# A gated cross-attention and FP4 feed-forward block on one core: gate and output projection computed with the weights stationary, turned back by PE, and the codes' casts given to DVE

## The chip, the cores and the metric

The kernel runs on one NeuronCore of a Trainium2 chip. The time is that of the device in microseconds (us), from start to end of the program. PE is TensorE, DVE is VectorE, ACT is ScalarE, POOL is GpSimd, SP is SyncE, whose queue issues the DMAs. PEld is PE's loading of the stationary operand.

## What is computed

```python
def _L0_xattn_ref(hidden_states, memory_tokens, memory_mask, norm_w, wq, wk, wv, wo, wg):
    x = rmsnorm(hidden_states, norm_w)
    q = (x @ wq.T).reshape(B, L, NH, HD)            # NH = 16 heads of HD = 32
    k = (memory_tokens @ wk.T).reshape(B, M, NH, HD)
    v = (memory_tokens @ wv.T).reshape(B, M, NH, HD)
    attn = jnp.einsum('blhd,bmhd->bhlm', q, k) * scale
    attn = jnp.where(memory_mask[:, None, None, :], attn, -jnp.inf)
    attn = jax.nn.softmax(attn, axis=-1)
    out = jnp.einsum('bhlm,bmhd->blhd', attn, v).reshape(B, L, C)
    out = out @ wo.T
    gate = jax.nn.sigmoid(x @ wg.T)
    return gate * out

def _L0_ffn_ref(x, ...):                            # weights are FP4 codes with group scales
    gate, up = halves of einsum('bsh,oh->bso', x, w_gu)
    h = jax.nn.silu(gate) * up
    y = jnp.einsum('bsi,hi->bsh', h, w_down)
    return y / jnp.sqrt(jnp.mean(y * y, axis=-1, keepdims=True) + EPS)

x = x + jnp.tanh(g_xattn[0]) * _L0_xattn_ref(_layernorm(x), ctx_2048, mask_BxS2_bk0, ...)
x = x + jnp.tanh(g_ffn[0]) * _L0_ffn_ref(_layernorm(x), ...)
```

There are 16 batches of 100 tokens of width 512, and 361 context tokens a batch, of which the mask leaves at most the last 96.

## The kernel before

**Split numbers.** Every fp32 operand of a product is kept as a high and a low part (fp32r, `_hi` and `_lo`), and a product is three passes: high by high, high by low, low by high. ACT copies the high part out of PSUM (`job_hi`), DVE subtracts it from the same bank and writes the low part (`job_lo`).

**Attention** takes four groups of NB = 4 batches, one after the other. A group is 16 steps, one for each head. In step i PE turns the probabilities of head i (`transpose_probs`, L1659), multiplies those of head i - 1 with the values (`attend`, L1673 and L1675), and in steps 2, 6, 10 and 14 computes the scores of the next four heads (`scores`). Beside that, each step does the jobs that the table `BESIDE` names for it, in its order, on PE, ACT and DVE alike:

- X0 to X3: the normalised tokens of batch n of the next group are turned (xT)
- Qn, Kn: 128 columns of the queries and keys of the group; W stationary (128 columns), tokens moving (400 of xT, 384 of the context)
- An, Bn: values for 128 context rows, half of the heads each
- Tn: the attention output of heads 4n to 4n + 3 is turned (oT)
- Gn: x @ wg for batch n, its 100 tokens stationary and 512 columns of wg moving, 12 matmuls; ACT then takes tanh of half of it into `gate[n]` (L902)
- On: the attention output of batch n by wo in the same manner, 12 matmuls (L1620, L1624). DVE then forms (gate + 1) * product (L1229) and that times a coefficient plus the residual (L1233), and SP stores it as x1.

A job's bank is in `BANK_OF` (and its variants for the first, third and last cycle); `open_bank` makes PE wait until the job before in that bank has been read. The loop over groups runs from step 6 of one group to step 5 of the next, three times, with steps 0 to 5 of group 0 ahead of it and steps 6 to 15 of group 3 behind it.

**FP4 weights** are decoded inside the three cycles of the loop, 6 pieces each (`KINDS = "uduudu"`). DVE does stages 0 to 2 (shift, mask, sign; L1317, L1326, L1333) for each, two stages a step behind `attn_sum`. Stage 3 of an up piece ("u", the codes of gate and up weights) is a cast of 128x1024 fp16 to fp32r by ACT (L953); stages 3 and 4 of a down piece ("d") are multiplications on POOL (L743). SP stores the result in DRAM scratch.

**Feed-forward.** Five groups (j) of 320 tokens, each 11 tiles (t) of 128 hidden columns. A tile is 16 matmuls for gate and up (L1771), whose banks ACT and DVE empty (L1037, L1395), POOL adds, and from j = 1 on the down products (L1784) of the group before. The first five tiles of j = 0 stand in steps 11 to 15 of the last attention group, the others in the order of `AT_LAST`, between the last O jobs. Tokens of the next j are normalised, turned in three pieces by PE (L1719), and split by ACT and DVE (L1367) within tiles of the present one; the first products of a j wait for the last split.

**POOL** also divides by the softmax sum (`attn_norm`, L733), takes rstd (L724) and forms the low part of the context of the next group (`ctx_lo`, L719), for which job K0 waits; ACT makes its high part at the steps of `CTX_AT`.

## Time and profile before

| | us |
|---|---|
| median of 3 runs | 585.15 (583.78 to 585.34) |
| the profiled execution, its own time | 583.25 |
| its span, first to last instruction | 581.4 |
| PE busy | 534.2 (92% of the span) |
| DVE busy | 431.1 (74%) |
| ACT busy | 347.9 (60%) |
| POOL busy | 295.7 (51%) |

A matmul's record holds its way through the array, so the records of neighbours overlap; what a matmul costs in a row of them is the distance from its start to the next one's start.

### The profile page before, as it was taken

Reading aid. Unit: us, or ns where it says so; the run is one execution under the profiler, and the core shown is the slowest. Engines: PE = TensorE matmul, PEld = TensorE weight load, DVE = VectorE, ACT = ScalarE, POOL = GpSimd, SP = SyncE. Lnnn points to the kernel's source line nnn. Section 1 sums busy time; section 2 is a strip of 40 time slices with the busy share of each in tenths; the row PEclk is TensorE's granted clock in tenths of the full one; section 3 lists DMA queues with packets and bytes.
Section 4 is the critical chain, followed back from the end, with each engine's and each line's share of the span. In section 5 each row is a group of like instructions: output and inputs, shape, how many; then the busy total and the mean of one; then the engine's idle time right before and its main releaser. Section 6 shows DMA issues by size and latency. Waiting matters only on the chain.

```text
span 581.4 us, 12493 instructions
## 1 busy us (share of the span) xinstructions
PE 534.2 (92%) x3962; PEld 468.0 (80%) x3962; DVE 431.1 (74%) x994; ACT 347.9 (60%) x948; POOL 295.7 (51%) x320
## 2 busy tenths in 40 slices
PE   2787988999899998999997898999999999999996
PEld 2687878988789887988886676888998988899983
DVE  6666868767688686896647987988897898867721
ACT  4677558645676446765467644676666667665610
POOL 6913373402735026441104854887776677866720
PEclk9998999999999999999999999999999999999998
DMA  6930146331464322432672027502110211011111
GB/s 223 340 118 0 56 130 184 135 135 49 147 168 159 117 65 93 147 132 92 220 277 76 2 61 238 195 0 83 38 36 2 83 37 37 2 37 37 37 64 32
DMA packets 27899, 59.37 MB, mean 102 GB/s; under 512 B 3656, under 2 KB 5832, under 8 KB 27848
## 3 DMA queue, kind: packets, MB, share of 16 engines
q1 hardware_dynamic: 27848, 58.76, 30.6%
q8 instruction: 23, 0.38, 0.3%
q14 instruction: 28, 0.23, 0.1%
HBM read 39.62 MB, written 19.14 MB: 101 GB/s over the span
## 4 chain that ended last, share of the span: by engine, by line
PE 64%; DVE 15%; issue 8%; ACT 8%; POOL 1%; DMA 1%; DVEq 0%; ACTq 0%; SPq 0%; POOLq 0%
PE bank L1771 18%; PE bank L1784 15%; PE bank L323 12%; PE bank L1620 5%; PE bank L1624 3%; PE bank L332 2%; ACT probs L928 2%; PE bank L1648 2%; DVE nmax L1206 2%; DVE vb_both L1174 2%; PE bank L1673 1%; PE bank L1659 1%; DVE part_gate L1395 1%; ACT vb_both L908 1%; DVE words L1317 1%
## 5 line engine op out<-in xcount | busy, mean ns | idle before, releaser
L1771 PE MATMUL bank<-mT_hi,wgu 128*128 128x320 f32 x440 | 138.3, 325 | 9.9 <-ACT part_up L1037 3.4
L1771 PE MATMUL bank<-mT_lo,wgu 128*128 128x320 f32 x440 | 131.2, 309 | 0.0
L733 POOL TENSOR_TENSOR o<-pv_sum,rinv 100x128 f32<-100x128 f32 x64 | 42.6, 666 | 147.4 <-DVE pv_sum L1223 147.2
L928 ACT ACTIVATE probs<-bank,nmax 100x96 f32<-100x96 f32 x256 | 66.6, 348 | 61.6 <-DVE nmax L1206 61.6
L1771 PEld LDWEIGHTS bank<-mT_hi,wgu 128*128 128x128 f32 x440 | 82.5, 188 | 23.5 <-ACT part_up L1037 5.2
L1771 PEld LDWEIGHTS bank<-mT_lo,wgu 128*128 128x128 f32 x440 | 82.7, 188 | 3.5
L805 POOL TENSOR_TENSOR part_gate<-part_gate 128x320 f32<-128x320 f32 x55 | 57.0, 1037 | 54.8 <-DVE part_gate L1395 54.8
L1037 ACT ACTIVATE part_up<-bank,scale 128x320 f32<-128x320 f32 x110 | 57.3, 522 | 39.9 <-PE bank L1771 39.6
L1395 DVE SCALAR_TENSOR_TENSOR part_up<-bank,scale,part_up 128x320 f32<-128x320 f32 x110 | 58.9, 546 | 20.0 <-ACT part_up L1037 18.5
L1037 ACT ACTIVATE part_gate<-bank,scale 128x320 f32<-128x320 f32 x110 | 52.1, 529 | 28.0 <-PE bank L1771 27.6
L1395 DVE SCALAR_TENSOR_TENSOR part_gate<-bank,scale,part_gate 128x320 f32<-128x320 f32 x110 | 55.4, 544 | 13.5 <-ACT part_gate L1037 11.8
L811 POOL TENSOR_TENSOR part_up<-part_up 128x320 f32<-128x320 f32 x55 | 57.4, 1044 | 8.7 <-DVE part_up L1395 7.1
L1784 PE MATMUL bank<-wdn_lo,hT_hi 128*128 128x512 f32 (+1 forms) x143 | 56.5, 395 | 0.0
L1784 PE MATMUL bank<-wdn_hi,hT_lo 128*128 128x512 f32 (+1 forms) x143 | 56.4, 395 | 0.0
L1784 PE MATMUL bank<-wdn_hi,hT_hi 128*128 128x512 f32 (+1 forms) x143 | 56.4, 394 | 0.0
L798 POOL TENSOR_TENSOR hT_lo<-hidden,hT_hi 128x320 fp32r<-128x320 f32 x55 | 50.4, 916 | 5.9 <-ACT hT_hi L1051 4.8
L1673 PE MATMUL bank<-vb_both,pT_hi 128*100 128x136 f32 x192 | 41.2, 290 | 0.0
L1206 DVE TENSOR_REDUCE nmax<-bank 100x4 f32<-100x384 f32 x64 | 35.3, 551 | 2.1 <-PE bank L1648 1.5
L1675 PE MATMUL bank<-vb_both,pT_lo 128*100 128x68 f32 x192 | 36.7, 219 | 0.0
L1051 ACT ACTIVATE hT_hi<-hidden 128x320 fp32r<-128x320 f32 x55 | 25.7, 467 | 17.6 <-DVE hidden L1410 17.6
L1211 DVE TENSOR_TENSOR pT_lo<-bank,pT_hi 128x300 fp32r<-128x300 f32 x64 | 29.8, 465 | 8.4 <-ACT pT_hi L936 7.3
L1659 PE MATMUL bank<-ident,probs 100*128 100x100 f32 x192 | 27.4, 252 | 6.3 <-DVE pT_lo L1211 6.3
...
## 6 DMA issues: line engine op xcount, KB each, us to landing
...
```

The costliest lines, as they stand in the source:

```text
L323: last = nc.tensor.matmul(out_ap, lhs(a, t), rhs(b, t), start=t == 0 and p == 0, stop=t == tiles - 1 and p == 2)
L733: nc.gpsimd.tensor_tensor(o[hg % 2][:, :, HD * h:HD * h + HD], total[:, :, 0:HD], rinv[:, i % 4, :].unsqueeze(2).broadcast_to([L, NB, HD]) ...
L798: nc.gpsimd.tensor_tensor(hT[t][LO][:, cols], hidden[n % 2][:, :], hT[t][HI][:, cols].bitcast(F32), ALU.subtract)\
L805: nc.gpsimd.tensor_tensor(a[:, :], a[:, :], b[:, :], ALU.add).then_inc(s_gate_sum, 1)
L811: nc.gpsimd.tensor_tensor(a[:, :], a[:, :], b[:, :], ALU.add).then_inc(s_up_sum, 1)
L928: last = nc.scalar.activation(probs[i % 2][:, cols], SC[i % HPG][0:L, cols], ACT.Exp, bias=nmax[:, i % 4, b:b + 1])
L1037: nc.scalar.activation(part[n % 2][i][k][:, :], product_bank(j, t, i, k)[:, 0:TG], ACT.Copy, scale=scale32[:, t, i, k:k + 1]).then_inc(s_e ...
L1206: nc.vector.tensor_reduce(nmax[:, i % 4, :], SC[i % HPG][0:L, 0:KC].rearrange("t (b k) -> t b k", b=NB), AXIS_X, ALU.max, negate=True).the ...
L1395: nc.vector.scalar_tensor_tensor(onto, product_bank(j, t, i, k)[:, 0:TG], scale32[:, t, i, k:k + 1], onto, ALU.mult, ALU.add).then_inc(s_e ...
L1673: nc.tensor.matmul(both[:, :, cols].rearrange("t a (b w) -> t a b w", w=VW), pT[i % 2][HI][:, c, :], vb_both[:, :, c, :, VW * i:VW * i + V ...
L1771: last = nc.tensor.matmul(product_bank(j, t, i, k)[:, 0:TG], wgu[t][:, k, 128 * i:128 * i + 128], mT[j % 2][half][:, k, :], start=half == ...
L1784: last = nc.tensor.matmul(bank[6 + slot][0:rows, :], hT[c][a][:, cols], wdn[c][b][:, :], start=c == 0 and p == 0, stop=c == FT - 1 and p == 2)
```

## The change

The gate and output projection are computed as Q and K are: W is stationary (128 output columns) and the 400 tokens of the whole group move. Job Gn or On now stands for 128 output columns of four batches, not for one batch. ACT's tanh goes to `gateT` and DVE's product (`gated_out`) to `gatedT`, both with the output columns on partitions. Four new jobs Y0 to Y3 turn `gatedT` back for one batch each (four transposes with the identity moving), and DVE's `output` adds the residual to that bank; SP stores x1 from the residual's tile. `BESIDE`, the bank tables, `CTX_AT`, `AT_LAST`, the tile at which the last piece for j = 1 is turned (10 for 9) and the use of bank 5 are other than before, residuals have four tiles and are loaded at the X jobs, and stage 3 of an up piece is a `tensor_copy` on DVE.

```diff
-        AT_LAST = ("H", 5, "T3", 6, "O0", "O1", 7, "O2", "O3", 8, 9, 10)
+        AT_LAST = ("H", 5, "T3", 6, "O0", "O1", 7, "O2", "O3", 8, "Y0", "Y1", 9, "Y2", "Y3", 10)
-        STATS_BESIDE_0, NORM_BESIDE_0, TURN_BESIDE_0 = (2, 3, 4), (5, 6, 7), (7, 8, 9)
+        STATS_BESIDE_0, NORM_BESIDE_0, TURN_BESIDE_0 = (2, 3, 4), (5, 6, 7), (7, 8, 10)
-            return (0, 2, 3) if n < 2 else (0, 2, 3, 4) if n < 8 else (0, 2, 3, 4, 5)
+            return (0, 2, 3) if n < 2 else (0, 2, 3, 4) if n < 10 else (0, 2, 3, 4, 5)
-        BESIDE = {0: ["Q1", "B0"], 1: ["K1", "T3", "B1"], 2: ["O0"], 3: ["O1", "B2"], 4: ["Q2", "O2"], 5: ["O3", "K2", "T0"],
-                  6: ["G0"], 7: ["Q3", "G1"], 8: ["K3", "X0"], 9: ["T1", "G2", "X1"], 10: ["G3", "X2"], 11: ["X3", "K0"],
-                  12: ["Q0"], 13: ["T2", "A0"], 14: ["A1"], 15: ["A2"]}
+        BESIDE = {0: ["Q1", "B0"], 1: ["K1", "T3", "B1"], 2: ["O0"], 3: ["O1", "O2"], 4: ["O3", "B2", "Q2"],
+                  5: ["T0", "K2", "Y0", "Y1", "Y2", "Y3"], 6: ["G0"], 7: ["Q3", "G1"], 8: ["K3", "G2"], 9: ["T1", "G3"],
+                  10: ["X0", "X1"], 11: ["X2", "X3", "K0"], 12: ["Q0", "A0"], 13: ["T2", "A1"], 14: [], 15: ["A2"]}
-        CTX_AT = {9: (0, 1), 10: (2, 3)}
+        CTX_AT = {8: (0,), 9: (1, 2), 10: (3,)}
...
-                    nc.scalar.activation(gate[n][:, :], src[0:L, :], ACT.Tanh, scale=0.5).then_inc(s_gate, 1)
+                    act.wait_ge(s_gated, NB * owner(c, name) + n + 1)
+                    nc.scalar.activation(gateT[:, n, :], src[:, 0:GT], ACT.Tanh, scale=0.5).then_inc(s_gate, 1)
...
+            def gated_out(g, n):
+                dve.wait_ge(s_gate, NB * g + n + 1)
+                dve.wait_ge(s_o, NB * g + n + 1)
+                dve.wait_ge(s_y, 1 + NB * g)
+                nc.vector.scalar_tensor_tensor(gatedT[:, n, :], gateT[:, n, :], 1.0, job_bank(g + 1, f"O{n}")[:, 0:GT],
+                                               ALU.add, ALU.mult).then_inc(s_gated, 1)
             def output(g, b):
+                dve.wait_ge(s_y, 1 + n + 1)
+                dve.wait_ge(s_xa[b], 16 * (g + 1))
+                nc.vector.scalar_tensor_tensor(residual[b], job_bank(g + 1, f"Y{b}")[0:L, :], coef_a[0:L, bass.ds(n, 1)], residual[b],
                                                ALU.mult, ALU.add).then_inc(s_x1, 1)
...
+                        nc.vector.tensor_copy(left[m % 2][:, :], code.bitcast(F16)).then_inc(s_left[KINDS[q]], 1)
...
-                    last = product(dst[0:L, :], lambda a, k: xT[a][:, k, L * n:L * n + L], lambda a, k: W["wg"][a][:, k, :], KT)
+                    last = product(dst[:, 0:GT], lambda a, k: W["wg"][a][:, k, 128 * n:128 * n + 128], lambda a, k: xT[a][:, k, :], KT)
                     last.then_inc(s_g, 1)
                     return
+                elif name[0] == "Y":
+                    pe.wait_ge(s_gated, NB * c + NB)
+                    for k in range(KT):
+                        last = nc.tensor.transpose(dst[0:L, 128 * k:128 * k + 128], gatedT[:, k, L * n:L * n + L], ident[:, :])
+                    last.then_inc(s_y, 1)
+                    return
...
-                        pe.wait_ge(s_gated, NB * (GROUPS + 1))
+                        pe.wait_ge(s_x1, NB * (GROUPS + 1))
                     transpose_tile(j + 1, m)
```

The wait on `s_x1` at the end of the diff is the one ahead of turning the third piece for j = 1: it now stands for the x1 of all four batches of the last group.

## Rows read from the trace of the kernel before

**Rows 1.** The page: busy time of each engine, and the granted clock in 40 slices
```profile
PE 534.2 (92%) x3962; PEld 468.0 (80%) x3962; DVE 431.1 (74%) x994; ACT 347.9 (60%) x948; POOL 295.7 (51%) x320
...
PEclk9998999999999999999999999999999999999998
```

**Rows 2.** Windows (busy PE, PEld, DVE, ACT, POOL; PEclk, DMA): one cycle, feed-forward
```profile
186.47:260.67 74.20, 70.53 (x650) 62.45 (x649) 56.53 (x141) 44.81 (x138) 28.37 (x29) 1.00 0.33 111
...
362.00:575.00 213.00, 209.93 (x1174) 185.60 (x1174) 161.99 (x348) 128.53 (x303) 145.00 (x152) 1.00 0.15 51
```

**Rows 3.** Waits of PE in that cycle: us in total, times, longest
```profile
PE bank L1659 <- DVE pT_lo L1211: 1.0, 1, 1.0
PE bank L1610 <- DVE kT_lo L1183: 0.9, 1, 0.9
PE bank L1599 <- DVE oT_lo L1185: 0.6, 1, 0.6
```

**Rows 4.** Timeline of PE (start, length, line): Q2 and then O2
```profile
195.24 0.34 PE L323 MATMUL bank<-xT_lo,wq_hi 128*128 128x400 f32 x1
...
197.06 0.34 PE L323 MATMUL bank<-xT_hi,wq_lo 128*128 128x400 f32 x1
197.24 0.39 PE L1620 MATMUL bank<-wo_hi,oT_hi 128*100 128x512 f32 x1
197.47 0.39 PE L1620 MATMUL bank<-wo_lo,oT_hi 128*100 128x512 f32 x1
...
199.09 1.10 PE L1624 MATMUL bank<-wo_hi,oT_lo 128*100 128x512 f32 x4
```

**Rows 5.** Timeline of PE: four transposes, 128 columns of the identity moving
```profile
293.88 0.60 PE L1719 MATMUL bank<-ident,mn 128*128 128x128 f32 x4
294.32 0.25 PE L1659 MATMUL bank<-ident,probs 100*128 100x100 f32 x1
```

**Rows 6.** Groups by line, ACT and DVE, the cycle from 186.47 to 260.67
```profile
L953 ACT ACTIVATE left<-fp 128x1024 fp32r<-128x1024 f16 x4 | 4.2, 1059 | 0.0
...
L1233 DVE SCALAR_TENSOR_TENSOR gate<-gate,coef_a,xa 100x512 f32<-100x512 f32 x4 | 3.0, 752 | 0.9 <-DVE gate L1229 0.7
L1229 DVE SCALAR_TENSOR_TENSOR gate<-gate,bank 100x512 f32<-100x512 f32 x4 | 2.8, 689 | 3.8 <-PE bank L1624 3.8
...
L1180 DVE SCALAR_TENSOR_TENSOR qT_lo<-bank,qT_hi 128x400 fp32r<-128x400 f32 x4 | 2.3, 575 | 2.2 <-ACT qT_hi L914 2.2
...
L1201 DVE TENSOR_SCALAR xn<-xn,mv,rstd 100x512 f32<-100x512 f32 x4 | 2.0, 538 | 0.0
...
L1321 DVE TENSOR_SCALAR scale_a<-scale 128x1024 int16<-128x1024 int16 x2 | 0.8, 419 | 0.0
```

**Rows 7.** Timelines of DVE and POOL: a shift on DVE beside a multiplication on POOL
```profile
256.52 1.51 DVE L1317 TENSOR_SCALAR words<-words,shift 128x512 int32<-128x512 int32 x1
...
255.61 2.14 POOL L743 TENSOR_TENSOR left<-fp,scale 128x1024 fp32r<-128x1024 f16 x1
```

**Rows 8.** Timeline of POOL in steps 9 to 11 of a group
```profile
225.10 2.13 POOL L743 TENSOR_TENSOR left<-fp,scale_a 128x1024 fp32r<-128x1024 f16 x1
227.38 1.98 POOL L719 TENSOR_TENSOR ctxT_lo<-ctx_raw,ctxT_hi 128x384 fp32r<-128x384 f32 x2
...
229.89 2.13 POOL L743 TENSOR_TENSOR left<-fp,scale 128x1024 fp32r<-128x1024 f16 x1
232.86 1.98 POOL L719 TENSOR_TENSOR ctxT_lo<-ctx_raw,ctxT_hi 128x384 fp32r<-128x384 f32 x2 [0.84 <-ACT ctxT_hi L893]
```

**Rows 9.** Timeline of ACT in step 15: the cast ahead of pT_hi
```profile
246.62 1.06 ACT L953 ACTIVATE left<-fp 128x1024 fp32r<-128x1024 f16 x1
247.71 0.42 ACT L936 ACTIVATE pT_hi<-bank 128x300 fp32r<-128x300 f32 x1
```

**Rows 10.** Timelines: PE enters tile 10 of j = 0, DVE ends tile 9
```profile
359.69 0.39 PE L1771 MATMUL bank<-mT_hi,wgu 128*128 128x320 f32 x1
...
361.53 0.49 DVE L1403 SCALAR_TENSOR_TENSOR hidden<-tgate,part_gate 128x320 f32<-128x320 f32 x1
```

More of the change, by code:

```diff
@@ L645, in _ @@
                     sp.sem_inc(s_x1st[b], 16)
-                for b in range(2):
-                    load_residual(0, b)
                 load_next(0)
@@ L656, in _ @@
                 load_gate_up(range(0, 4))
+                for b in range(NB):
+                    load_residual(GROUPS - 1, b)
                 sp.wait_ge(s_pj, split_count(GROUPS - 1, "Q3"))
@@ L667, in _ @@
                 load_down(range(1, 2))
+                sp.wait_ge(s_o, NB * GROUPS)
+                load_down(range(2, 6))
+                next_x1(2)
                 for b in range(NB):
-                    output(GROUPS - 1, b, True)
-                    if b == 1:
-                        for other in range(NB):
-                            sp.wait_ge(s_x1st[other], 64)
-                        next_x1(2)
-                load_down(range(2, 10))
+                    output(GROUPS - 1, b)
                 for b in range(NB):
@@ L961, in step @@
                 for job in beside(g, i):
-                    if job[1][0] != "O":
+                    if job[1][0] not in "OY":
                         job_hi(*job)
-                if cycle is not None:
-                    for q, stage in DECODE_AT.get((i, 1), ()):
-                        if stage > 2 and KINDS[q] == "u":
-                            piece_left(cycle, q, stage - 3)
                 if last and i in TURNED_AT:
@@ L1137, in _ @@
                     act.wait_ge(f_g, b + 1)
-                    nc.scalar.activation(gate[0][:, :], FJ[0:L, :], ACT.Tanh, scale=0.5).then_inc(f_gate, 1)
+                    nc.scalar.activation(gateT[0:L, :, 0:128], FJ[0:L, :].rearrange("t (k c) -> t k c", k=KT), ACT.Tanh, scale=0.5).then_inc(f_gate, 1)
                 act.wait_ge(f_gate, B)
-                with act.Fori(0, GROUPS - 1) as g:
-                    for q, stage in STAGES:
-                        if stage > 2 and KINDS[q] == "u":
-                            piece_left(g, q, stage - 3)
                 phase_barrier(act)
@@ L1577, in open_bank @@
                     pe.wait_ge(s_gated, NB * c + n + 1)
+                elif other[0] == "Y":
+                    pe.wait_ge(s_x1, NB * c + n + 1)
                 else:
```

108 lines of the change are left out of this document (57 added, 51 removed).

## The prediction

> **What bounds the kernel now.** I read the page's busy shares first. PE is busy 92% of the span and the granted clock is at the upper of its two levels (2.4 GHz) in nearly all slices [rows 1], so no gain hides in the clock. The windows say where the other 8% lie: one cycle of the loop (a group's 16 steps) takes 74.20 us, with PE busy for 70.53, DVE for 56.53, ACT for 44.81 and POOL for 28.37; the feed-forward from 362 us on has PE busy 209.93 of 213.00 [rows 2]. Both are PE's. In the loop 74.20 - 70.53 = 3.67 us of a cycle are PE's idle time, and its waits name DVE: pT_lo 1.0, kT_lo 0.9, oT_lo 0.6 us [rows 3]. So PE sets the time, and DVE, at 76% of a cycle, is what PE now and then waits for. DMA plays no part: the waits of PE in this cycle hold none.
>
> **What a projection costs PE.** A G or O matmul (512 columns moving) starts 0.23 us after the one before it; a Q matmul (400 columns, 128 stationary, the very shape that G and O take) 0.18 to 0.19 us [rows 4]. From 195.24 to 197.24 there are 11 distances of Q, from there to 199.09 there are 8 of O [rows 4], that is 0.182 and 0.231: 0.049 us less for each. A group has 2 x 4 x 12 = 96 of them, so PE saves 96 x 0.049 = 4.7 us a group, 18.8 in all.
>
> The Trainium skill's page "TensorE: Matmul & The Clock Gate" (section "Back-to-back issue gap") gives for streams of weight load and matmul 131 ns at 512 columns and 81 ns at 128, that is 0.13 ns a column. By that 112 columns fewer would be worth 15 ns, 5.6 us in the 384 matmuls. The rows have 0.23 us at 512, so the trace disagrees.
>
> **What Y costs PE.** Four transposes with 128 identity columns moving took 294.32 - 293.88 = 0.44 us [rows 5]; the bounds are 0.34 (the same with 100 columns, as in T) and 0.44. I take 0.40: 1.6 us a group, 6.4 in all. PE's own work thus falls by 4.7 - 1.6 = 3.1 us a group, 12.4 in all.
>
> **DVE and ACT.** A cast by ACT is 1.06 us, four a cycle [rows 6]; it leaves ACT and comes to DVE. A copy of this shape on DVE isn't in the trace. From below it costs 0.42 (128x1024 int16 in and out, L1321), from above twice the 128x512 fp32 form of L1201, 1.08 [rows 6]; it writes fp32, so I take 0.8: 3.2 us a cycle on DVE (1.7 to 4.3). The four first products of `gate` shrink from 0.69 (L1229) to about 0.58, as L1180 with 400 columns out of PSUM, and the four second ones (L1233, 0.75) now read PSUM as L1229 does, 0.69 [rows 6]: 0.7 us less a cycle. DVE has 56.5 + 3.2 - 0.7 = 59.0 us in a cycle of some 71: still below PE, but 83% and in order. ACT has room (44.8 - 4.2).
>
> DVE's shift of the words took 1.51 us where it began inside a multiplication by POOL, which ran from 255.61 to 257.75; it took 0.42 to 0.48 elsewhere [rows 7]. The page "SBUF — State Buffer" of the Trainium skill (section "SBUF: two separate sides") calls this an exclusive lock: a DVE operation in a two-port mode and one on POOL shut each other out for their whole length. By that a cast that meets a down piece on POOL would lose up to 2.1 us. Here the casts stand in steps 7, 12, 14 and 2 and the down pieces in 9, 10 and 0, so I put nothing for it.
>
> **What the order does to PE's waits.** Gone: kT_lo (0.9), since T1 has another bank than K3, and the oT_lo wait of X3. The pT_lo wait of 1.0 at step 0 came after ACT's cast at 246.62, which held pT_hi back until 247.71 [rows 9]; the cast moves to DVE, in front of that same subtraction. Steps 13 to 15 lose A1 to A0's shift forward (13 and 14 have T2, A1 and nothing), so PE has less to do there than DVE: about 6.8 against 10 us. Half of that is hidden by the step that DVE may lag; I put 2.0 us of wait for it (was 1.5).
> New are these. Y3 uses Y0's bank, and DVE empties it only after K2's low half (ACT 0.5, DVE 0.5) and its own 0.69: 0.6 us beyond the 1.2 us of Y0 to Y2. K0 needs the context's low halves. From the start of the first down piece to the end of the fourth half POOL works 2.13 + 1.98 + 0.6 (L733) + 2.13 + 0.99 = 7.8 us if three halves are left behind it [rows 8], while PE's steps 9 and 10 shrink from about 11.5 us to 6.0 (G2, X0, X1 and waits left them); K0's first eight matmuls cover 1.5. I get a wait of 1.3 us. Smaller ones at scores and X2 make 1.0. Sum of waits: 2.0 + 0.6 + 1.3 + 1.0 = 4.9, against 4.3 by start-to-start distances now (3.67 by busy time). **A cycle:** 74.2 - 3.1 + 0.6 = 71.7, that is 2.5 less, three times: -7.5.
>
> **Last group and tail.** Its G jobs give 48 x 0.049 = 2.35; its steps 10 to 15 are partly bound by ACT and DVE emptying banks, so I take -2.0. Its O jobs give -2.35, its Y jobs +1.6: -0.75. The order of the tail costs. PE's turning of the third piece now stands behind Y2 and Y3 and waits until DVE has done Y3's output. In the run shown PE ended tile 9 at 359.69, and DVE ended its part at 361.53 + 0.49 = 362.0 [rows 10], 2.3 us later. To that come two outputs of 0.69: 3.7, of which Y2 and Y3 on PE cover 0.8, so PE stands 2.9 us. Tile 10 is then the only cover for the split: the next j's first products wait until DVE has done tile 10 (2.3 behind) and the split of 64 rows (0.4), near 2.1 us after covers. While PE stands the banks come free, and tile 10 takes about 2.4 us of dense matmuls for 3.7 now. Sum 2.9 + 2.1 - 1.3 = 3.7; bank 5 from tile 10 on only makes it no less. I take +3.5. The rest of the feed-forward is as before: loads of the down weights now stand before and after the stores of x1, but the first late one (tile 6) is wanted at the fourth tile of j = 1, more than 10 us on. Residual loads (16 as before) come a dozen us ahead. Steps 0 to 5 of group 0 have no O job either way: 0.
>
> **Sum.** -7.5 - 2.0 - 0.75 + 3.5 = -6.75 on the profiled execution's 583.25, 576.5. That one stood 1.9 below the median of the runs shown, 585.15, so the median comes to 578.4; I say 578.3.
>
> **Rivals.**
> - *The waits go as well.* With ACT free of casts and fewer bank conflicts PE's waits fall to 2 us a cycle, and the tail's stall to half: 3 x (3.1 + 2.3) + 2.75 - 1.7 = 17.2 less, 568. For it: three of the waits now are of conflicts that the new tables lack [rows 3]. Against it: DVE gets 3 us more. 0.20.
> - *DVE becomes the bound in stretches.* The cast at 1.08, in steps 7 and 14 where DVE already has more than PE, and every us late there is a us of PE. 2.5 more of waits a cycle takes all the cycle's gain: 585.15 - 2.75 + 3.5 = 586, and with half of it 582. 0.14 for 581.5 to 586.9.
> - *POOL holds K0* (the other side). If DVE's locks stretch POOL's pieces (its divisions took 0.40 us alone and up to 1.8 beside decoding), and the last half comes 3.5 us later than I put it, a cycle takes 75.2: three times +1.0, with the tail +0.75: 589. It decides from 2.3 us beyond my 1.3. 0.12.
> - *The projections don't get cheaper*: were a 128-wide load the pace, G and O would stay at 0.231, and Y, waits and tail would add 6.4 + 1.8 + 3.5, 597. Q's 0.18 at this very shape speaks against it [rows 4]. 0.02.
> - *My forecast*, 571 to 581.5: 0.52.
> The page on TensorE named above is a milder form of the last one: 5.6 saved, 595 - 4 = 591; the 0.23 us of the rows leaves it no chance of its own.
>
> **Chances.** A measurement of this kernel can tell about 0.3% (1.75 us) from no change. Faster are my case, the first rival and two thirds of the second's lower half: 0.52 + 0.20 + 0.07 = 0.79, less 0.02 for what I haven't seen: 0.77. Within 0.3%: 0.08. Slower: 0.15. The range 568 to 586 leaves out the far ends of the first and third rival and the fourth; my case alone has 571 to 581.5.
>
> **What would show it.** Right: G and O matmuls 0.18 apart, Y near 0.4 us a job; a cycle of 71 to 72.5 us; PE waiting for DVE around step 0, and K0 (L336) for ctxT_lo by POOL; L1719 in tile 10 waiting 2 to 3 us for DVE's output. Wrong: a cast over 1.1 us, a cycle of 74, or a cycle under 70 with DVE over 88% busy and PE hardly waiting. The prediction falls if DVE's lag at steps 13 to 15 or POOL's at step 11 is much unlike what I laid out by hand, which is its weakest part; the projections' price is its firmest.

## The result, and the profile after

| | before | after |
|---|---|---|
| median of the runs, us | 584.87 (583.78 to 585.34, 4 runs) | 590.19 (589.66 to 592.54, 4 runs) |
| ratio, 95% interval | | 1.0093 [1.0068, 1.0118] |
| the profiled execution, us (span) | 583.25 (581.4) | 589.96 (588.2) |

The kernel became 0.9% slower; the forecast was 1.1% faster. The profiled execution of the kernel before stands 1.6 us below the median of its runs, that of the kernel after 0.2 below, so the profiles differ by 6.8 us where the medians differ by 5.3. The page of the kernel after, busy time and granted clock (compare [rows 1]):

```profile
PE 540.8 (92%) x4026; PEld 499.9 (85%) x4026; DVE 435.9 (74%) x1006; ACT 337.7 (57%) x936; POOL 297.6 (51%) x320
...
PEclk9896999999799997889999999899999999999999
```

The busy shares hardly differ from before. The last line does: TensorE is at the lower of its two levels (1.2 GHz) in seven stretches besides the end, 48.4 us by the clock records of the trace, against 6.3 us before. That profile of the kernel before is a good one: over 25 runs of it beside e5 to e8 the mean granted clock was 0.978 to 0.995, median 0.981, and the profile has 0.995; the four runs of the kernel after have 0.959 to 0.971. By these means (an estimate: twice what is missing to 1, times the span) the low clock is some 22 us in the median run before, and some 34 to 48 after.

Cutting the span at the first transposes of step 6 of each group, where the loop's cycles begin, and at those of the very last step, shows where the time went. The last column is what the prediction gave for the change.

| stretch | before | after | change | us at 1.2 GHz after | forecast |
|---|---|---|---|---|---|
| start, to step 5 of group 0 | 57.60 | 59.29 | +1.7 | 17.1 | 0 |
| loop cycle 1 | 74.21 | 73.10 | -1.1 | 0 | -2.5 |
| loop cycle 2 | 74.21 | 74.43 | +0.2 | 6.8 | -2.5 |
| loop cycle 3 | 74.21 | 76.00 | +1.8 | 13.7 | -2.5 |
| last group, steps 6 to 14 | 43.61 | 43.03 | -0.6 | 3.4 | -2.0 |
| last step, tail and feed-forward | 257.56 | 262.34 | +4.8 | 7.5 | +2.75 |
| span | 581.4 | 588.2 | +6.8 | 48.4 | -6.75 |

Before, these stretches hold 3.4 us at 1.2 GHz in the start and 2.9 at the very end, and none between. The same loop body took 73.10, 74.43 and 76.00 us, so what differs between its cycles is no work, but waits and the clock. In the rest of the text "group 1" and "group 2" are the 16 steps from step 0 to step 15 of these groups.

**The projections did become cheaper.** Timeline of PE after, an O job of 12 matmuls (start, length, line):

```profile
117.73 0.34 PE L1633 MATMUL bank<-oT_hi,wo_hi 128*128 128x400 f32 x1
...
119.19 0.90 PE L1637 MATMUL bank<-oT_lo,wo_hi 128*128 128x400 f32 x4
```

Eight distances from 117.73 to 119.19 are 0.182 us each, where before they were 0.231 [rows 4]. Groups by line in groups 1 and 2 of after, 100.58 to 250.59, give the other prices (busy us, mean ns of one, idle before):

```profile
L1316 DVE TENSOR_SCALAR fp<-words 128x512 int32<-128x512 int32 x13 | 7.9, 605 | 0.5
...
L1334 DVE CAST left<-fp 128x1024 fp32r<-128x1024 f16 x8 | 5.5, 688 | 0.5
...
L1624 PE MATMUL bank<-ident,gatedT 128*100 128x128 f32 x32 | 4.6, 278 | 0.6 <-DVE kT_lo L1168 0.6
...
L1215 DVE SCALAR_TENSOR_TENSOR gatedT<-gateT,bank 128x400 f32<-128x400 f32 x8 | 4.6, 570 | 8.9 <-issue 5.3 <-PE bank L1637 3.6
```

The cast took 0.69 us (I had put 0.8), gated_out 0.57 (0.58). The Y jobs cost more than forecast. Timeline of PE at the end of loop cycle 1:

```profile
129.79 1.03 PE L1624 MATMUL bank<-ident,gatedT 128*100 128x128 f32 x8
131.13 1.30 PE L1624 MATMUL bank<-ident,gatedT 128*100 128x128 f32 x8 [0.30 <-DVE kT_lo L1168]
132.39 0.47 PE L1672 MATMUL bank<-ident,probs 100*128 100x100 f32 x3
```

From 129.79 to 132.39 are 2.60 us, 0.30 of it a wait: 0.57 us a job where I had 0.40, so 2.3 us a cycle for 1.6.

**Where the cycle lost it again.** Windows of the kernel after: the three loop cycles, then group 1 split into steps 0 to 8 and 9 to 15 (us, then PE, PEld, DVE, ACT, POOL, PEclk, DMA share and GB/s):

```profile
59.29:132.39 73.10, 69.06 (x666) 66.20 (x664) 58.96 (x146) 41.35 (x135) 28.78 (x29) 1.00 0.34 122
132.39:206.82 74.43, 71.39 (x666) 69.16 (x665) 59.93 (x145) 40.97 (x134) 28.39 (x29) 0.95 0.39 129
206.82:282.82 76.00, 73.79 (x665) 71.66 (x665) 58.96 (x145) 41.39 (x134) 28.34 (x29) 0.91 0.31 103
100.58:147.14 46.56, 45.99 (x401) 44.70 (x402) 36.29 (x91) 23.31 (x77) 13.69 (x16) 1.00 0.29 106
147.14:175.01 27.87, 25.39 (x265) 24.43 (x263) 23.65 (x55) 17.67 (x59) 14.68 (x14) 0.88 0.53 170
```

From one cycle to the next PE is 2.3 and 2.4 us longer busy with the same work and 1.0 and 0.8 us less idle, so a stretch of 6.8 us at 1.2 GHz costs 1.3 to 1.6 us net. The same halves of the kernel before:

```profile
100.36:145.81 45.45, 45.26 (x377) 39.99 (x378) 35.00 (x87) 24.69 (x78) 12.78 (x16) 1.00 0.34 115
145.81:174.56 28.75, 25.27 (x274) 22.45 (x272) 21.53 (x55) 20.17 (x62) 15.59 (x14) 1.00 0.50 154
```

Steps 0 to 8 are PE's in both, almost without waits: 1.1 us longer, since the Y jobs and G2 lie there now, against six cheaper jobs. Steps 9 to 15 lost G2 (12 x 0.231 = 2.8 us) and 0.6 us of G3, and got X0 (0.4): 3.0 us less. They are 0.9 shorter. In them DVE is busy 23.65 of 27.87 us (85%, before 75%), and the granted clock has fallen to 0.88. What PE waits for in them (us in total, times, longest):

```profile
PE bank L1672 <- DVE pT_lo L1196: 1.8, 3, 0.9
PE bank L1651 <- DVE oT_lo L1170: 0.6, 1, 0.6
```

DVE's timeline in step 11, and POOL's beside it:

```profile
157.27 0.46 DVE L1196 TENSOR_TENSOR pT_lo<-bank,pT_hi 128x300 fp32r<-128x300 f32 x1
...
157.93 1.62 DVE L1316 TENSOR_SCALAR fp<-words 128x512 int32<-128x512 int32 x1
159.58 0.77 DVE L1323 SCALAR_TENSOR_TENSOR fp<-words,fp 128x512 int32<-128x512 int32 x1
160.28 1.04 DVE L1162 TENSOR_TENSOR xT_lo<-bank,xT_hi 128x400 fp32r<-128x400 f32 x2
```
```profile
156.16 2.13 POOL L743 TENSOR_TENSOR left<-fp,scale 128x1024 fp32r<-128x1024 f16 x1
158.25 1.01 POOL L719 TENSOR_TENSOR ctxT_lo<-ctx_raw,ctxT_hi 128x384 fp32r<-128x384 f32 x1
```

The mask of the codes (L1316) took 1.62 us where it met POOL's work; it took 0.419 in a run where POOL's pieces were thin (below), and 0.92 at this place before. The subtractions that PE's next jobs need stand behind it. And the clock is low from 154.0 to 160.9. That is ahead of the three waits for pT_lo (they end at 168.78, 171.95 and 175.01) and 1.8 us behind the one for oT_lo, which ends at 152.23. The low clock makes K0 slow (timeline of PE, two matmuls of 384 columns):

```profile
158.06 0.52 PE L336 MATMUL bank<-ctxT_hi,wk_lo 128*128 128x384 f32 x1
158.38 0.52 PE L336 MATMUL bank<-ctxT_hi,wk_hi 128*128 128x384 f32 x1
```

They start 0.32 us apart; in loop cycle 1, at full clock, it is 0.18. No wait of PE for the context's low halves (POOL) is listed in these cycles. K0's last four matmuls, which need them, take 1.05 us in loop cycle 1 and 0.70 before, so such a wait is 0.35 us at most.

**Where the tail lost it.** Timeline of PE around tiles 9 and 10 of j = 0; the bracket is idle time before, and its releaser:

```profile
359.42 0.41 PE L1785 MATMUL bank<-mT_hi,wgu 128*128 128x320 f32 x1 [2.08 <-DVE part_gate L1396]
360.28 1.03 PE L1624 MATMUL bank<-ident,gatedT 128*100 128x128 f32 x8
364.02 0.43 PE L1733 MATMUL bank<-ident,mn 64*128 64x64 f32 x4 [2.71 <-DVE xa_more L1222]
369.54 0.63 PE L1785 MATMUL bank<-mT_hi,wgu 128*128 128x320 f32 x1 [1.57 <-DVE mT_lo L1368]
```

DVE in that stretch:

```profile
357.51 1.39 DVE L1222 SCALAR_TENSOR_TENSOR xa<-bank,coef_a,xa 100x512 f32<-100x512 f32 x2
...
362.48 1.40 DVE L1222 SCALAR_TENSOR_TENSOR xa_more<-bank,coef_a,xa_more 100x512 f32<-100x512 f32 x2
```

Tile 9 waits 2.08 us, since DVE does the outputs of Y0 and Y1 ahead of the additions that free its banks; the third piece of tokens waits 2.71 for the outputs of Y2 and Y3, as forecast; the first products of j = 1 wait 1.57 for its split. The clock is low from 365.7 to 372.5, while tile 10 and those products run.

### The profile page after: what moved, and what is told of

It reads as the page before. It is cut to its first block, busy times and chain, and to the rows that moved or that the text cites. A ratio compares the mean times of both kernels' runs of the same rounds, so it can differ in the third digit from the quotient of the medians.

```text
span 588.2 us, 12644 instructions
## 1 busy us (share of the span) xinstructions
PE 540.8 (92%) x4026; PEld 499.9 (85%) x4026; DVE 435.9 (74%) x1006; ACT 337.7 (57%) x936; POOL 297.6 (51%) x320
## 4 chain that ended last, share of the span: by engine, by line
PE 67%; DVE 15%; issue 8%; ACT 6%; DMA 1%; POOL 1%; DVEq 1%; SPq 0%; ACTq 0%; POOLq 0%
PE bank L1785 20%; PE bank L1798 15%; PE bank L327 13%; PE bank L1633 4%; PE bank L1661 2%; PE bank L336 2%; PE bank L1637 2%; PE bank L1686 2%; PE bank L1672 2%; ACT probs L927 2%; DVE nmax L1191 2%; DVE stats L1176 1%; DMA xn<-in_x 1%; PE bank L1733 1%; PE bank L1688 1%
## 5 line engine op out<-in xcount | busy, mean ns | idle before, releaser
L1785 PE MATMUL bank<-mT_hi,wgu 128*128 128x320 f32 x440 | 139.9, 328 | 12.4 <-DVE part_gate L1396 3.3
L1785 PE MATMUL bank<-mT_lo,wgu 128*128 128x320 f32 x440 | 133.4, 314 | 0.0
L1785 PEld LDWEIGHTS bank<-mT_hi,wgu 128*128 128x128 f32 x440 | 84.2, 191 | 24.4 <-DVE part_gate L1396 5.7
L1785 PEld LDWEIGHTS bank<-mT_lo,wgu 128*128 128x128 f32 x440 | 84.7, 193 | 3.5
L1024 ACT ACTIVATE part_up<-bank,scale 128x320 f32<-128x320 f32 x110 | 57.4, 522 | 42.2 <-PE bank L1785 40.9
L1686 PE MATMUL bank<-vb_both,pT_hi 128*100 128x136 f32 x192 | 43.6, 300 | 0.0
L1688 PE MATMUL bank<-vb_both,pT_lo 128*100 128x68 f32 x192 | 38.8, 228 | 0.0
L935 ACT ACTIVATE pT_hi<-bank 128x300 fp32r<-128x300 f32 x64 | 27.1, 423 | 19.9 <-PE bank L1672 19.5
L1159 DVE TENSOR_TENSOR vb_both<-bank,vb_both 32x256 fp32r<-32x256 f32 (+2 forms) x56 | 23.6, 421 | 18.3 <-ACT vb_both L907 17.6
L1672 PE MATMUL bank<-ident,probs 100*128 100x100 f32 x192 | 29.0, 262 | 8.4 <-DVE pT_lo L1196 8.4
```

The source lines that it names most:

```text
L1024: nc.scalar.activation(part[n % 2][i][k][:, :], product_bank(j, t, i, k)[:, 0:TG], ACT.Copy, scale=scale32[:, t, i, k:k + 1]).then_inc(s_e ...
L1686: nc.tensor.matmul(both[:, :, cols].rearrange("t a (b w) -> t a b w", w=VW), pT[i % 2][HI][:, c, :], vb_both[:, :, c, :, VW * i:VW * i + V ...
L1688: last = nc.tensor.matmul(both[:, 0, cols].rearrange("t (b w) -> t b w", w=VW), pT[i % 2][LO][:, c, :], vb[HI][:, c, :, VW * i:VW * i + VW ...
L1785: last = nc.tensor.matmul(product_bank(j, t, i, k)[:, 0:TG], wgu[t][:, k, 128 * i:128 * i + 128], mT[j % 2][half][:, k, :], start=half == ...
```

## The experiments

My theory after the result: the forecast price of the projections is right, but PE's saving is in steps where DVE, in order and with the casts and the collisions with POOL, is what PE waits for, and the clock falls behind such waits (this last part the runs bear out only in part, see below). Rivals: the casts cost what they cost wherever they stand; the clock alone takes the time; the collisions alone do it; the projections give nothing. Times are medians; each ratio is to runs of the kernel before on the same chip. Runs of one kernel spread by 3 to 8 us, so that the single profiles are used for stretches and the ratios for the whole.

| run | median, us | ratio to before | group 1 | group 2 | last group, 15 steps | last step to end | us at 1.2 GHz |
|---|---|---|---|---|---|---|---|
| before | 585.2 to 585.3 | 1 | 74.20 | 74.21 | 75.07 | 257.6 | 6.3 |
| after | 590.19 | 1.0093 | 74.43 | 75.58 | 75.27 | 262.3 | 48.4 |
| e1_filler | 589.08 | 1.0075 [1.0044, 1.0106] | 74.00 | 76.06 | 74.87 | 261.5 | 24.5 |
| e2_casts_act | 587.04 | 1.0026 [1.0008, 1.0045] | 73.99 | 74.19 | 74.59 | 263.1 | 40.9 |
| e3_tail | 589.02 | 1.0046 [1.0018, 1.0075] | 74.51 | 75.66 | 75.23 | 260.9 | 47.0 |
| e4_spread | 589.52 | 1.0070 [1.0043, 1.0098] | 76.12 | 74.76 | 74.73 | 262.4 | 34.7 |
| e5_before_casts_dve | 583.49 | 0.9984 [0.9963, 1.0005] | 73.90 | 73.93 | 75.04 | 257.5 | 16.9 |
| e6_thin_dve | 578.92 | 0.9911 [0.9874, 0.9947] | 71.33 | 71.56 | 73.95 | 260.7 | 20.3 |
| e7_thin_pool | 586.69 | 1.0038 [1.0011, 1.0065] | 71.37 | 72.12 | 74.23 | 263.0 | 37.6 |
| e8_tail_early | 589.11 | 1.0062 [1.0032, 1.0092] | 74.31 | 74.89 | 74.66 | 261.2 | 46.6 |
| e9_before_thin_dve | 581.75 | 0.9937 [0.9907, 0.9967] | 73.43 | 73.41 | 74.56 | 257.5 | 15.5 |
| e10_tail_both | 586.87 | 1.0035 [1.0013, 1.0056] | 74.27 | 75.72 | 75.23 | 258.4 | 48.0 |
| e11_act_tail | 582.74 | 0.9962 [0.9944, 0.9979] | 73.95 | 74.19 | 74.60 | 259.0 | 33.4 |
| e12_act_spread_tail | 582.67 | 0.9944 [0.9923, 0.9965] | 73.14 | 74.63 | 74.63 | 258.3 | 26.7 |

The same profiles by the loop's own cycles, from step 6 to step 5; in brackets the us at 1.2 GHz within:

| run | start, to step 5 of group 0 | cycle 1 | cycle 2 | cycle 3 |
|---|---|---|---|---|
| before | 57.6 (3.4) | 74.21 (0) | 74.21 (0) | 74.21 (0) |
| e5 | 58.6 (13.7) | 73.91 (0) | 73.90 (0) | 73.94 (0) |
| e9 | 60.0 (13.7) | 73.43 (0) | 73.41 (0) | 73.41 (0) |
| after | 59.3 (17.1) | 73.10 (0) | 74.43 (6.8) | 76.00 (13.7) |
| e3 | 60.9 (17.1) | 73.13 (0) | 74.64 (6.8) | 75.88 (13.7) |
| e8 | 59.6 (17.1) | 74.06 (3.4) | 74.64 (6.8) | 74.32 (6.8) |
| e10 | 56.5 (10.2) | 75.89 (13.7) | 74.01 (3.4) | 75.93 (13.7) |
| e1 | 56.5 (10.2) | 73.23 (0) | 76.02 (3.4) | 73.74 (0) |
| e2 | 56.8 (10.2) | 73.10 (0) | 74.48 (6.8) | 73.38 (3.4) |
| e11 | 57.7 (10.2) | 73.05 (0) | 74.45 (6.8) | 73.38 (3.4) |
| e4 | 59.9 (17.1) | 74.78 (3.4) | 75.31 (3.4) | 73.23 (0) |
| e12 | 61.2 (17.1) | 72.68 (0) | 74.70 (3.4) | 72.31 (0) |
| e7 | 61.0 (17.1) | 72.08 (0) | 71.38 (0) | 71.99 (0) |
| e6 | 58.1 (6.8) | 71.30 (0) | 70.57 (0) | 71.59 (3.4) |

The start differs by 4.4 us between e3 and e10, whose code is the same there, so I read nothing from it. After, e3, e8 and e10 have the same loop, for only their tails differ: twelve cycles of one code. They took 73.1 us without low clock, 74.0 to 74.1 with 3.4 us of it, 74.3 to 74.6 with 6.8, and 75.9 to 76.0 with 13.7. That is 0.2 us for each us at 1.2 GHz, and it holds at one place as well: cycle 1 alone took 73.10, 73.13, 74.06 and 75.89. At full clock the changed cycle is thus 1.1 us shorter than the old one, not 2.5, and the clock takes that away.

**e1_filler**: PE gets work that depends on nothing, where it is thin. Does the clock alone take the time?

```diff
+            FILL = {"S3": 5, "A1": 3, "S0": 5, "A2": 4}
+
+            def fill(c, name, dst):
+                for r in range(0 if isinstance(c, int) else FILL.get(name, 0)):
+                    nc.tensor.matmul(dst[:, 0:400], W["wg"][HI][:, r % KT, 0:128], W["wg"][HI][:, r % KT, 0:400], start=True, stop=True)
```

It is called ahead of the job and writes into the job's own bank, for the scores into bank 4: 17 matmuls a cycle.

> The changed kernel with 17 more matmuls of 400 columns a cycle on PE (loop only), put where PE waits for DVE: 5 into bank 4 ahead of the scores in steps 10 and 14, 3 ahead of A1, 4 ahead of A2; their results are overwritten and enter nothing. They are 3.1 us more work for PE in each of three cycles. Theory clock (the projections cost what was forecast, but steps 10 to 15 are now so thin for PE that its granted clock falls to 1.2 GHz, and the work that follows at half speed eats the gain): the clock stays up in the loop, K0 takes 2.1 us for 3.7, a cycle takes 71.5 to 73 us for 74.4 and 75.6, the time falls by 4 to 8 us from 590.2. Rival DVE-bound (PE waits for DVE and the clock is beside the point): the waits just fill, the time stays within 1.5 us or grows by up to 9.

Measured: 589.08, 1.1 us under the changed kernel, as the rival had it. Windows of groups 1 and 2:

```profile
97.82:171.82 74.00, 71.92 (x683) 68.71 (x682) 59.67 (x146) 40.97 (x136) 27.61 (x29) 1.00 0.37 127
171.82:247.88 76.06, 73.26 (x683) 70.12 (x682) 60.40 (x146) 40.99 (x136) 28.00 (x29) 0.98 0.35 118
```

In group 1 the clock never fell, and it took 74.00. The loop's cycles say more. Loop cycle 1 has full clock with and without filler, and took 73.23 and 73.10: 17 x 0.18 = 3.1 us more work for PE cost 0.1 us, so it went into time in which PE waits. What sets that cycle is what PE waits for, and full clock alone doesn't bring the 71.7 us of the forecast. In cycle 3 the clock stayed up with the filler, and it took 73.74 for 76.00. Cycle 2 lost the gain again: step 2 of group 2 took 7.18 us, with low clock from 184.2 to 187.6.

**e2_casts_act**: the casts go back to ScalarE, all else as after.

```diff
-        DECODED_BY = dict(u="dve", d="pool")
+        DECODED_BY = dict(u="act", d="pool")
```

> The changed kernel with the casts of the up codes back on ACT. Theory clock: DVE loses 4 x 0.6 us a cycle, the waits at steps 12 to 15 shrink by 0.5 to 1 us a cycle, but ACT's casts hold pT_hi back as before; steps 10 to 13 stay thin, the clock still falls; within 2 us of 590.2. Rival (the casts on DVE cost the time): 3 to 6 us faster.

Measured: 587.04, 3.2 us under the changed kernel: the rival's lower end. The casts on DVE are a cost in this order. The profiles say by which way: loop cycles 1 and 2 took 73.10 and 74.48, as with the casts on DVE (73.10 and 74.43), and cycle 3 took 73.38 for 76.00, with 3.4 us at 1.2 GHz for 13.7. At full clock the casts cost nothing that these profiles show; they cost where low clock comes with them. e11, which has the same loop as e2, repeats its three times within 0.05 us.

**e3_tail**: Y2 and Y3 of the last group go to banks 6 and 7, so that the third piece of tokens is turned without waiting for their outputs.

```diff
-        ... O2=1, O3=5, Y0=1, Y1=5, Y2=1, Y3=5)}
+        ... O2=1, O3=5, Y0=1, Y1=5, Y2=6, Y3=7)}
...
-                        pe.wait_ge(s_x1, NB * (GROUPS + 1))
+                        pe.wait_ge(s_x1, NB * GROUPS + 1)
```

> The changed kernel with Y2 and Y3 of the last group in banks 6 and 7, so that the turning of the third piece for j = 1 waits for Y0's output only and not for Y3's. Theory: PE's wait of 2.98 us ahead of tile 10 goes, and with it the clock's fall at 366 us, under which tile 10 and the first products of j = 1 ran; 4 to 6 us faster than 590.2. Rival (DVE's part of the tail is the bound, and the wait only moves to the split of the third piece): under 1.5 us faster.

Measured: 589.02, 1.2 us under the changed kernel, as the rival had it. The wait of 2.71 ahead of L1733 is gone, and PE waits 2.7 us for the split of that piece (mT_lo) at the first products of j = 1 instead. The tail got 1.4 us shorter, of 4.8 lost. Moving one wait was not enough, since DVE's queue stayed as long.

**e4_spread**: A0 and A1 one step later, so that step 14 isn't empty.

```diff
-                  ... 12: ["Q0", "A0"], 13: ["T2", "A1"], 14: [], 15: ["A2"]}
+                  ... 12: ["Q0"], 13: ["T2", "A0"], 14: ["A1"], 15: ["A2"]}
```

> The changed kernel with A0 and A1 one step later each, as in the kernel before (A0 in step 13, A1 in step 14, where the change has none), nothing else. Theory clock: PE's load in steps 12 to 15 is more even; the fall of the clock in steps 15 and 0 goes, the one in steps 10 and 11 stays: 1 to 3 us faster than 590.2. Rival (only DVE's total there counts): within 1 us.

Measured: 589.52, 0.7 us under the changed kernel, as the rival had it. Steps 9 to 15 fell from 27.86 and 29.02 us to 27.34 and 26.79, but in group 1 step 2 grew from 4.93 to 7.08: DVE's mask of the codes collided there with a piece of POOL,

```profile
109.05 2.15 DVE L1316 TENSOR_SCALAR fp<-words 128x512 int32<-128x512 int32 x1
108.42 2.50 POOL L743 TENSOR_TENSOR left<-fp,scale 128x1024 fp32r<-128x1024 f16 x1 [0.85 <-DMA gate_up_scratch<-left]
```

and PE waited 0.9 us for kT_lo behind it and ran the next job at half clock. Whether a collision falls ahead of something that PE wants is a matter of a microsecond in the order, and it cost 2 us here.

**e5_before_casts_dve**: the kernel before with the casts on DVE alone.

```diff
-                            if stage < 3:
+                            if stage < 3 or KINDS[q] == "u":
                                 decode(cycle, q, stage)
...
+                elif not down:
+                    nc.vector.tensor_copy(left[m % 2][:, :], code.bitcast(F16)).then_inc(s_left[KINDS[q]], 1)
```

> The kernel before, its order and projections untouched, with the twelve casts of the gate and up codes on VectorE. Theory that the casts hurt because the new order leaves VectorE with too little room in steps 9 to 15: in the old order they fall into longer steps, so at most 2 us more than before (585 to 587 us), granted clock 0.99. Rival, a cast on VectorE costs the same in either order (putting them back on ScalarE gave back 0.7 per cent of the changed kernel): 588.5 to 590 us.

Measured: 583.49, ratio 0.9984, as the theory has it and against the rival. A window of the length of one cycle:

```profile
175.00:249.00 74.00, 70.57 (x649) 62.54 (x650) 59.38 (x146) 41.46 (x136) 28.47 (x29) 1.00 0.37 122
```

DVE is as busy as after (59.4 of 74), and PE's clock is full. The same casts that cost 3.2 us after the change cost nothing before it. The share of busy time didn't tell the two apart; the order of the steps did.

**e6_thin_dve** and its control **e9_before_thin_dve**: DVE's decoding on one sixteenth of its columns, in the new and in the old order.

```diff
-nc.vector.tensor_copy(left[m % 2][:, :], code.bitcast(F16)) ...
+nc.vector.tensor_copy(left[m % 2][:, 0:64], code[:, 0:32].bitcast(F16)) ...
-nc.vector.tensor_scalar(word[:, :], word[:, :], shift[:, 0:1], ...
+nc.vector.tensor_scalar(word[:, 0:32], word[:, 0:32], shift[:, 0:1], ...
```

> The changed kernel, with VectorE's four operations on each piece of codes (shift, mask, sign, cast) on one sixteenth of the columns, so that only the issue and the waits of them are left; the weights of the second phase are then wrong. Theory that VectorE's queue sets the pace of the thinned steps and that TensorE's clock falls because of these waits: each cycle loses the waits and most of the low clock, 71 to 72.5 us a cycle instead of 74.4 and 75.6, some 578 to 582 us in all, mean clock 0.98 or more. Rival, the clock falls by what TensorE itself does there whatever VectorE does: cycles of 73.5 us and more, over 585 us, clock 0.96 to 0.97.

> The control for thin work on VectorE: the kernel before, with VectorE's three operations on each piece of codes (shift, mask, sign) on one sixteenth of the columns; its casts stay whole on ScalarE; the weights of the second phase are wrong. Theory that VectorE holds up the new order and not the old one, and that the cheaper projections are then worth what was forecast: the cycle stays at 73.5 to 74.2 us (thin after: 71.3 and 71.6), 582 to 585 us in all. Rival, any kernel of this kind gains 11 us when VectorE is relieved, and the projections give nothing: cycles of 71 to 72 us, 575 to 578 us.

Windows of e6: group 1, and its steps 9 to 15:

```profile
97.39:168.72 71.33, 68.40 (x665) 66.00 (x665) 51.29 (x145) 40.87 (x135) 23.16 (x29) 1.00 0.39 134
...
144.16:168.72 24.56, 22.34 (x265) 21.26 (x263) 16.39 (x52) 17.61 (x59) 12.03 (x13) 1.00 0.55 183
```

and of e9:

```profile
147.43:175.85 28.42, 25.26 (x273) 22.48 (x272) 18.75 (x55) 20.13 (x62) 12.31 (x14) 1.00 0.51 158
102.42:147.43 45.01, 45.01 (x378) 39.81 (x378) 32.64 (x88) 24.55 (x78) 10.76 (x16) 1.00 0.34 114
```

Relieving DVE took 3.1 and 4.0 us from groups 1 and 2 of the new order, and 0.8 from those of the old one. A part of this is the low clock that went too: loop cycle 1, at full clock in all four kernels, lost 1.8 us in the new order (73.10 to 71.30) and 0.8 in the old (74.21 to 73.43). With DVE out of the way the change is worth 73.43 - 71.33 = 2.1 us in group 1 and 1.85 in group 2: the projections' saving is there. Steps 9 to 15 are where the relief counts: 27.87 to 24.56 in the new order, 28.75 to 28.42 in the old. e6 was at the good end of what the theory gave. e9's whole time came out under my 582, and its ratio says that the old order too gains 0.6% from a lighter DVE; groups 1 to 3 account for 2.1 us of that. In e9 the casts stay whole on ACT, so the pair also differs in ACT's work.

**e7_thin_pool**: GpSimd's multiplications of the down pieces on one sixteenth of their columns; DVE's work is whole.

```diff
-nc.gpsimd.tensor_tensor(left[m % 2][:, :], code, (scale_a, scale)[r][:, :], ALU.mult) ...
+nc.gpsimd.tensor_tensor(left[m % 2][:, 0:64], code[:, 0:64], (scale_a, scale)[r][:, 0:64], ALU.mult) ...
```

> The changed kernel, with GpSimd's multiplications of the down pieces on one sixteenth of their columns; VectorE's work is complete, the weights of the second phase are wrong. Theory that VectorE is late by its own work, and that collisions with GpSimd add only 1 to 2 us a cycle: 585 to 588 us. Rival, collisions between the two are the chief cause of VectorE's lateness: the same as with thin work on VectorE, 578 to 582 us. If neither engine's pieces matter: 589 to 590 us.

The window of group 1, and DVE's mask in groups 1 and 2:

```profile
101.73:173.10 71.37, 68.47 (x664) 65.99 (x665) 56.67 (x145) 40.91 (x136) 21.44 (x29) 1.00 0.39 135
```
```profile
L1318 DVE TENSOR_SCALAR fp<-words 128x512 int32<-128x512 int32 x12 | 5.0, 419 | 0.5
```

The whole, 586.69, is what my theory had. The cycles aren't: the loop's three took 72.08, 71.38 and 71.99 us, all at full clock, near those with thin work on DVE (71.30, 70.57, 71.59), which is what the rival had. DVE's busy time in them fell from 58.96, 59.93 and 58.96 to 57.37, 56.68 and 57.29 though it does the same work. So the collisions lengthen its work by 1.6 to 3.3 us a cycle, 2.2 on average: over the three cycles the mask takes 0.62 on average for 0.42, 1.62 at the worst place above, and the shift 0.68 for 0.53. The kernel before had such collisions too, but fewer: shift and mask took 6.9 us a cycle in it, 7.8 after and 5.6 in e7. In the loop, then, DVE is late by the collisions as much as by its own work: taking away either is nearly enough. Loop cycle 1, at full clock in both, gives the price of the collisions alone: 73.10 against 72.08, 1.0 us. In the other two the low clock went with the collisions, and their gains of 3.1 and 4.0 us can't be divided between them. The whole gained less because this profile has more low clock than e6 in the start (17 us against 7) and in the tail, where no pieces are decoded.

The Trainium skill's page "SBUF — State Buffer" (section "SBUF: two separate sides") says that a DVE operation in a two-port mode and one of GpSimd exclude each other for their whole length. The trace agrees: the mask takes 0.42 us alone, 1.62 beside POOL's 2.13 and 1.01, and 2.15 beside its 2.50 in e4, and in both places it ends 0.3 us after POOL's piece.

**e8_tail_early** and **e10_tail_both**: the tail in other orders. In both, all output projections stand behind tile 6.

The second line is that of e8 and the third that of e10, which also has the banks and waits of e3:

```diff
-        AT_LAST = ("H", 5, "T3", 6, "O0", "O1", 7, "O2", "O3", 8, "Y0", "Y1", 9, "Y2", "Y3", 10)
+        AT_LAST = ("H", 5, "T3", 6, "O0", "O1", "O2", "O3", 7, "Y0", "Y1", 8, "Y2", "Y3", 9, 10)
+        AT_LAST = ("H", 5, "T3", 6, "O0", "O1", "O2", "O3", 7, "Y0", "Y1", 8, 9, "Y2", "Y3", 10)
...
-        ... TURN_BESIDE_0 = (2, 3, 4), (5, 6, 7), (7, 8, 10)
+        ... TURN_BESIDE_0 = (2, 3, 4), (5, 6, 7), (7, 8, 9)
```

> The changed kernel with only the tail's order changed: all four output projections stand behind tile 6, the first two turned pieces behind tile 7 and the other two behind tile 8, and the third piece of the next token group is turned beside tile 9 as in the kernel before. Theory that the tail loses 4.7 us because turned pieces and residual additions stand between tiles 8 and 10, just ahead of the split for the next token group: the waits of 2.4 and 2.98 us go, the stretch of low clock at 365.7 too, 585.5 to 587.5 us; from the last transposes to the end 258 to 259.5 us instead of 262.3. Rival, VectorE has the same work in this stretch and only waits elsewhere: 588.5 us or more, 261 us or more in the tail.

> The changed kernel with a tail in which no turned piece stands before the split of the next token group: four output projections behind tile 6, Y0 and Y1 behind tile 7, tiles 8 and 9, then Y2 and Y3 in banks 6 and 7, tile 10; the third piece of tokens is turned beside tile 9 and waits for Y0's residual addition alone. Theory that the 4.7 us of the tail come from the wait for residual additions ahead of that turning and from the low clock behind it: from the last transposes to the end 257 to 259 us, 585 to 587 us in all. Rival, the tail is late by the additional work itself: 261 us or more, 588 to 590 us in all.

e8 met the rival, at 589.11: the wait only went to where the third piece is turned (PE's timeline),

```profile
361.18 0.66 PE L1733 MATMUL bank<-ident,mn 64*128 64x64 f32 x4 [3.83 <-DVE xa_more L1222]
```

and the tail took 261.2 us. In e10, at 586.87, nothing that the next token group needs stands behind a Y job's output, and the tail took 258.4: 3.9 of the 4.8 us were the order. The stretch from tile 6 to the second tile of j = 1 in before, after and e10 (one window of each kernel, in this order):

```profile
332.70:367.90 35.20, 31.93 (x166) 24.42 (x164) 28.93 (x54) 18.11 (x43) 18.52 (x20) 1.00 0.54 173
```
```profile
334.70:374.70 40.00, 32.50 (x181) 29.06 (x180) 28.66 (x54) 18.65 (x43) 18.61 (x20) 0.91 0.42 135
```
```profile
334.20:370.40 36.20, 31.21 (x182) 27.01 (x181) 28.04 (x54) 18.39 (x43) 18.46 (x20) 1.00 0.35 111
```

Busy times are alike in all three. What differs is which wait stands ahead of what, and the clock that follows.

**e11_act_tail** (e10 and e2 together) and **e12_act_spread_tail** (e4 too):

> The tail of the kernel above and the casts back on ScalarE; all else as in the changed kernel. If the two add up (3.2 us for the casts, 3 to 4 for the tail): 582 to 584 us, cycles of 74 us, and so about as fast as the kernel before or slightly faster. Rival, low clock moves from one stretch to another and takes back a part: 585 to 587 us.

> As the kernel above, with the values' products A0 and A1 one step later (steps 13 and 14), so that no step stands without a projection. Theory that the waits for the probabilities' low halves in steps 13 to 15 go where PE has other work there: cycles of 72.5 to 73.5 us, 578 to 582 us in all, faster than the kernel before. Rival, the wait moves to K1's low half in step 2, as where the spreading was done alone: cycles of 74 to 76 us, 583 us or more.

e11 came to 582.74: the two gains add up, and the kernel is 0.4% faster than before. e12 came to 582.67, ratio 0.9944, the best of those that compute everything, if not distinguishable from e11. Steps 9 to 15 took 25.93 and 25.86 us in it, and the clock was full in group 1, 73.14 us. In group 2 the rival came in: step 2 took 7.19 us, with a wait of 1.0 us for kT_lo and low clock from 186.8 to 190.2. Windows of the two groups:

```profile
101.47:174.61 73.14, 68.52 (x664) 65.93 (x665) 56.55 (x141) 44.52 (x139) 28.05 (x29) 1.00 0.38 130
174.61:249.24 74.63, 70.01 (x664) 67.43 (x665) 56.59 (x141) 44.56 (x139) 28.75 (x29) 0.98 0.36 123
```

Step 2 alone prices the two kinds of loss: 4.44 us without a wait (e7, and group 2 of e11), 5.58 with the wait (group 1 here), 7.19 with the wait and the low clock behind it.

So the change of the projections does pay, 2.6 us by the medians of the 6.75 forecast, with an order and a division of work that the changed kernel doesn't have.

## Why the prediction was wrong

- **What a projection costs: right.** 0.182 against 0.231 us a matmul, and 1.9 to 2.1 us in groups 1 and 2 of e6 against e9, where the terms gave 3.1 - 0.6 = 2.5. **What Y costs was too low:** 0.57 us a job where I had taken 0.40, 0.7 us a cycle. My source was a single row of four transposes [rows 5].
- **The loop: -7.5 forecast, +0.9 measured.** I had a cycle at 71.7 us, and the three took 73.10, 74.43 and 76.00: 8.4 us too much. The first has full clock, so by my estimate from it about 1.4 us a cycle, 4.2 in all, are missed without the clock, and the other 4.2 come with its falls (1.3 in the second cycle, 2.9 in the third). Two steps of the prediction failed, one for each half.
- **"So I put nothing for it": the step that failed at full clock.** The sentence is about casts that meet POOL's pieces. I looked only at whether the new casts would meet them. The rest of the decoding meets them as well, and when steps 9 to 15 shrink, there is less room between DVE and PE to hide it. Without the collisions (e7) the three cycles took 72.08, 71.38 and 71.99, at the forecast's 71.7; in the first, like for like, they cost 1.0 us. This and Y's 0.7 are more than the 1.4, since the wait of 1.3 us for K0 that I had forecast hardly came (0.35 at most). DVE's busy time in a cycle I had at 59.0, and it was 58.96, 59.93 and 58.96: the amount was right, but not what I took from it, that DVE has room because it stays below PE.
- **"So no gain hides in the clock": true, but a loss did, and this step carries the other half.** I read the full clock [rows 1] as a property of the kernel, put its loss at nothing and didn't ask what kept it up. The changed kernel has 20.5 us at 1.2 GHz in its three cycles, the one before none. By twelve cycles of the same loop each us of that costs 0.2 us. Step 2 in e12's groups (7.19 against 5.58) puts a price of 1.6 us on one stretch of 3.4 us, more than that average.
- **The cast's price: right, its place wrong.** 0.69 us each where I took 0.8. Nothing in the old order (e5), 3.2 us in the new (e2), and there by the low clock of the third cycle, not by the casts' own time.
- **"What the order does to PE's waits": the place right, what follows not.** PE is short of work in steps 13 to 15 while DVE isn't: three waits for pT_lo, 1.8 us, where I had 2.0, and a smaller wait at the scores (0.6). A wait was counted at its own length alone. In group 1 the clock fell 1.8 us behind the wait at the scores, in group 2 behind that one and again at the wait of 0.9 for pT_lo in step 15. But the same waits for pT_lo (0.9 and 0.6 us) in steps 15 and 0 of loop cycles 1 and 2 were not followed by low clock, nor was the 1.0 of the kernel before. So the waits are not a sufficient condition, and no rule comes out of these traces.
- **Last group, steps 6 to 14: -2.0 forecast, -0.6 measured.** The G matmuls had covered the split of the last token piece. PE's timeline has the first products of tile 0 wait 1.17 us for it, and then the clock is low for 3.4 us (307.6 to 311.0):

```profile
306.41 0.41 PE L1785 MATMUL bank<-mT_hi,wgu 128*128 128x320 f32 x1 [1.17 <-DVE mT_lo L1368]
```

  My text had it ("partly bound by ACT and DVE emptying banks"), with 0.35 us taken off for it.
- **Tail: +2.75 forecast, +4.8 measured.** The wait for Y3's output was 2.71 (I had 2.9) and that for the split 1.57 (2.1). Missing was the wait of 2.08 in tile 9, behind the outputs of Y0 and Y1 on DVE; and instead of 1.3 us given back by dense matmuls in tile 10 the clock fell for 6.8 us.
- **The rivals.** "DVE becomes the bound in stretches" was the mechanism, at 0.14; it was held down by putting its price at 582 to 586, as if DVE's lateness cost only its own length. "POOL holds K0" had the right sign with the wrong mechanism: no wait for the context's low halves appeared, but POOL did the harm through DVE.
- **Slips in the text.** The last rival's "595 - 4 = 591" should read 597 - 5.6; the result is the same. DVE's shift "took 0.42 to 0.48 elsewhere": it never took less than 0.47, and the 0.42 is the mask's.

What stays open is what makes the clock fall. Every experiment that removed the waits lifted the clock too, and one that filled them (e1) lifted it too, so the two hang together; but equal waits in equal cycles were followed by low clock in one and not in another. The split of the loop's miss into 4.2 us and 4.2 rests on single profiles. Nor was the low clock in the start, 6.8 to 17 us in the other profiles and 3.4 in that of before, traced to a cause.
